# Attention and feed-forward layer: where two V products stand in the even heads

## What is computed

```
x = L0_attn_x
xn = _layernorm(x, axis=-1)
x = x + _L0_attn_ref(xn, Wq, bq, Wk, bk, Wv, bv, Wo, bo) + _L0_ffn_ref(xn, gate, up, down and their scales)

q = (x @ Wq + bq).reshape(b, h, t, dh)
k = (x @ Wk + bk).reshape(b, t, h, dh).transpose(0, 2, 3, 1)
v = (x @ Wv + bv).reshape(b, t, h, dh).transpose(0, 2, 1, 3)
logits = jnp.einsum('bhtd,bhds->bhts', q, k) * scale
weights = jax.nn.softmax(logits + mask, axis=-1)       # causal mask
out = jnp.einsum('bhts,bhsd->bhtd', weights, v)
return out.transpose(0, 2, 1, 3).reshape(b, t, h * dh) @ Wo + bo
```

## Time and profile before

| | |
|---|---|
| median of three runs | 1229.3 us |
| the profiled execution, its own time | 1229.01 us |
| its span, first to last instruction | 1227.2 us |
| TensorE matmuls busy | 1213.9 us (99%) |
| VectorE busy | 858.6 us (70%) |
| ScalarE busy | 746.6 us (61%) |
| GpSimd busy | 747.2 us (61%) |
| TensorE on the chain that ended last | 92% |
| granted TensorE clock | 1.0 |

### The profile page before, as it was taken

How to read it: one execution, slowest core, us unless ns; L and a number is a source line. 1 busy time by engine, 2 the same in 40 slices (tenths; PEclk the granted TensorE clock), 3 DMA queues, 4 the chain that set the end, 5 groups by cost and what they waited for, 6 DMA issues and landing times.

```text
span 1227.2 us, 20579 instructions
## 1 busy us (share of the span) xinstructions
PE 1213.9 (99%) x7556; PEld 1077.2 (88%) x7556; DVE 858.6 (70%) x1674; ACT 746.6 (61%) x1548; POOL 747.2 (61%) x796
## 2 busy tenths in 40 slices
PE   9999999999999999999999999999999999999998
PEld 8888888888889898889999988899898889899987
DVE  7777777776677666766677766677666766677775
ACT  6644444444576667666667765676666666666764
POOL 7445555553576767446767772676767446767763
PEclk9999999999999999999999999999999999999999
DMA  7100000000000001110000012010001100000001
GB/s 170 32 7 14 14 14 7 27 1 9 14 13 14 17 23 31 35 31 14 27 14 14 14 31 65 14 48 14 14 27 31 48 1 13 27 14 14 14 6 35
DMA packets 57346, 29.86 MB, mean 24 GB/s; under 512 B 16288, under 2 KB 57248, under 8 KB 57248
## 3 DMA queue, kind: packets, MB, share of 16 engines
q1 hardware_dynamic: 55888, 27.49, 8.1%
q10 hardware_dynamic: 1360, 1.06, 0.3%
HBM read 26.44 MB, written 2.10 MB: 23 GB/s over the span
## 4 chain that ended last, share of the span: by engine, by line
PE 92%; ACT 2%; POOL 2%; DVE 2%; issue 1%; DVEq 0%; ACTq 0%; POOLq 0%
PE ps L41 27%; PE ps L43 27%; PE ps L42 27%; PE ps L1164 10%; PE ps L1026 1%; PE ps L1005 1%; DVE pt_lo L877 1%; POOL probs L736 1%; ACT q_all L413 0%; ACT pt_hi L491 0%; ACT probs L505 0%; ACT wq_hi L403 0%; POOL wq_lo L622 0%; POOL inv_sum L733 0%; DVE probs L958 0%
## 5 line engine op out<-in xcount | busy, mean ns | idle before, releaser
L736 POOL TENSOR_TENSOR probs<-probs,inv_sum 128x128 f32<-128x128 f32 (+7 forms) x256 | 293.6, 1147 | 20.1
L733 POOL TENSOR_TENSOR inv_sum<-row_sum,minus_one 128x1 f32<-128x1 f32 x256 | 140.5, 549 | 225.2 <-ACT probs L505 224.2
L505 ACT ACTIVATE probs<-probs,neg_max 128x128 f32<-128x128 f32 (+7 forms) x256 | 198.8, 777 | 92.2 <-DVE neg_max L958 90.3
L491 ACT ACTIVATE pt_hi<-ps 128x512 fp32r<-128x512 f32 (+3 forms) x384 | 173.7, 488 | 93.0 <-PE ps L1164 90.4
L877 DVE TENSOR_TENSOR pt_lo<-ps,pt_hi 128x512 fp32r<-128x512 f32 (+3 forms) x384 | 200.9, 551 | 16.0 <-ACT pt_hi L491 15.8
L958 DVE CUSTOM_DVE_ANT_0 probs<-ps,mask_row 128x128 f32<-128x128 f32 (+7 forms) x256 | 192.1, 750 | 6.4
L1164 PE MATMUL ps<-ident,probs 128*128 128x128 f32 x1152 | 168.7, 273 | 4.1 <-DVE pt_lo L877 2.1
L717 POOL TENSOR_TENSOR hid_lo<-act_buf,hid_hi 128x512 fp32r<-128x512 f32 x64 | 82.7, 1293 | 139.3 <-ACT hid_hi L445 139.3
L1164 PEld LDWEIGHTS ps<-ident,probs 128*128 128x128 f32 x1152 | 133.7, 141 | 17.4 <-issue 7.2
L43 PE MATMUL ps<-pt_hi,v_lo 128*128 128x512 f32 (+3 forms) x386 | 133.0, 345 | 0.0
L42 PE MATMUL ps<-pt_lo,v_hi 128*128 128x512 f32 (+3 forms) x386 | 132.9, 344 | 0.0
(11 more groups left out here) (154 smaller groups left out, 3377.1 us busy)
## 6 DMA issues: line engine op xcount, KB each, us to landing
wq_in<-in_wq SPq DMA_DIRECT2D x63, 128.0 KB, 2.4
kv_in<-in_wk SPq DMA_DIRECT2D x16, 256.0 KB, 2.6
wo_in<-in_wo SPq DMA_DIRECT2D x32, 128.0 KB, 2.1
kv_in<-in_wv SPq DMA_DIRECT2D x32, 128.0 KB, 2.4
out<-acc SPq DMA_DIRECT2D x7, 256.0 KB, 2.6
acc<-in_x SPq DMA_DIRECT2D x2, 512.0 KB, 5.4
raw<-in_gate SPq DMA_DIRECT2D x16, 64.0 KB, 1.8
raw<-in_up SPq DMA_DIRECT2D x16, 64.0 KB, 2.0
```

The lines of the kernel that those rows point to most:

```text
L491: nc.scalar.activation(pt_blocks(pt_hi, i, ch), T[at % 2][:, 0:blocks * P].rearrange("p (a b) -> p a b", b=P), ACT.Copy).then_inc(pt_hi_do ...
L505: nc.scalar.activation(row, row, ACT.Exp, bias=neg_max[:, s % 16:s % 16 + 1], scale=-1.0, accum_out=row_sum[:, s % 16:s % 16 + 1]).then_in ...
L733: nc.gpsimd.tensor_tensor(inv_sum[:, at], row_sum[:, at], minus_one[:], ALU.pow).then_inc(inv_done, 1)
L736: nc.gpsimd.tensor_tensor(row, row, inv_sum[:, at].to_broadcast([P, (tile_of(h, i) + 1) * P]), ALU.mult).then_inc(probs_done, 1)
```

## The change

In the even heads V0 moves from EARLY to LATE in step 4, behind the probabilities' products, and V1 moves from LATE in step 4 to EARLY in step 5, behind that step's scores. In head 30 V1 moves in the same way, and K1+ moves from EARLY to LATE in step 5, directly behind V1. The order of the jobs among each other stays.

```diff
-        EVEN = {0: {EARLY: "K0"}, 1: {FIRST: "K1"}, 2: {EARLY: "O0a"}, 3: {LATE: "O0b"}, 4: {EARLY: "V0", LATE: "V1"},
+        EVEN = {0: {EARLY: "K0"}, 1: {FIRST: "K1"}, 2: {EARLY: "O0a"}, 3: {LATE: "O0b"}, 4: {LATE: "V0"}, 5: {EARLY: "V1"},
                 6: {FIRST: "O1a"}, 7: {FIRST: "O1b"}}
...
-        JOBS[NH - 2] = {**EVEN, 5: {EARLY: "K1+"}, 6: {EARLY: "O1a"}, 7: {EARLY: "O1b"}}
+        JOBS[NH - 2] = {**EVEN, 5: {EARLY: "V1", LATE: "K1+"}, 6: {EARLY: "O1a"}, 7: {EARLY: "O1b"}}
```

## The result

The change makes the kernel slower: 1249.3 us, the median of four runs (1249.15 to 1249.78), against 1229.15 us before. The ratio is 1.0164, with a 95% interval from 1.0152 to 1.0176. Forecast were 1248.0 us and a range of 1244.4 to 1252.5. The profiled execution of after took 1249.15 us with a span of 1247.3, so 20.1 us more than that of before.

A forecast was written before the change was run, and what follows sets the result against it. TensorE bounds the kernel, by its work plus its waits. Waits of 19.9 us in 14 heads and 1.6 in head 30, less 2.5 gained, add 19.0 to 1229.0: 1248.0 us, range 1244.4 to 1252.5.

The forecast's parts named there:

- The gain: Heads 6, 14 and 22: V0 no longer waits 0.82 us for GpSimd's vw_lo, 2.5 us saved in all.
- the three waits: V0's waits for GpSimd's vw_lo in heads 6, 14 and 22, 0.82 us each, forecast to go.
- The copy of 1.58 us: From the slot behind a V product to the next product on shared bank M, ScalarE and VectorE free: 1.58 us.
- Waits A and B: Even heads, bank M: V1 waits 0.20 us behind V0 (A), O1a waits 1.22 us behind V1 (B).
- The sum: Waits of 14 heads 19.9 us, head 30 1.6, less gain 2.5: net +19.0 us.
- The upper bound: 1252.5 us, if bank M's copy takes 1.73 us instead of 1.58 at both waits of 14 heads and head 30.
- The busy time: TensorE's busy time stays near 1214 us while the span grows to about 1246.
- The copies did not stay hidden: Faster rival: bank M's copies stay hidden, only the vw_lo wait goes, 1226.5 us; chance 0.05 together with a mixed case.
- The copy did not queue behind the maximum of the scores: Slower rival: VectorE's maximum comes ahead of V1's v_lo, 0.95 us in each of 15 heads, 1262 us; chance 0.07.
- The clock did not fall: Rival: TensorE from O1a to head's end runs at 1.2 GHz in 15 heads, about 1318 us; chance 0.02.
- The rule on short idle spells: Skill page's warning: short idle spells from waiting for PSUM buffers can let TensorE's clock swing between two levels.
- The low bound: 1244.4 us, if half of the 7.2 us that 20 transposes waited with their weight loads went.

The follow-up runs named there:

- clearing GpSimd's queue alone: Kernel before, with splits of the next group's first Q weights moved from steps 1 and 3 to steps 3 and 5: 1226.2 us, ratio 0.9978.
- V1 ahead of the scores: The change with V1 moved ahead of step 5's scores, and K1+ in head 30 behind them: 1249.56 us, ratio 1.0168.
- V0 back: The change with V0 returned to its old place, EARLY in step 4, V1 and K1+ left as moved: 1247.44 us, ratio 1.015.
- the bank of its own: The change with V1 of heads 2 to 30 written to bank O instead of bank M, no instruction moved: 1230.7 us, ratio 1.0013.

## Why the prediction was right

*The gain.* 2.5 us were forecast from the earlier trace rows; the three waits are gone, and clearing GpSimd's queue alone gives 2.8 us (by the interval of its ratio, 1.6 to 3.8). Right.

*The copy of 1.58 us.* It was read at one place, head 30, and is 1.57 us at both places in head 4 of after. That ScalarE and VectorE are free in time was worked out from durations; the 1.05 us that VectorE idled before the second v_lo show it. Right, with 0.3 us more to spare than counted.

*Waits A and B.* 0.20 and 1.22 us forecast, 0.19 and 1.21 measured. K1+ waits 1.6 us as forecast. Their sum over the heads is the 22.1 us in the list of weight loads, 15 x 0.24 + 14 x 1.21 + 1.61; the rows of the weight loads count wait A as 0.24 us, where the starts give 0.19.

*The sum.* 19.0 us forecast, 20.1 measured in the profiled executions. The two waits of head 4 are 1.40 us together where 1.42 were forecast, 0.3 us less in 14 heads. What the sum lacked is that the products do not keep their lengths. In head 4 V1 takes 437.66 - 436.15 = 1.51 us where it took 1.45 before (432.97 to 434.42), and O1a takes 0.82 us (439.23 to 440.05, where the next scores start) where it took 0.79 in the kernel before (436.16 in the earlier trace rows to 436.95):

```profile
436.95 0.40 PE L41 MATMUL ps<-k_hi_even,q_hi 128*128 128x512 f32 x1
```

Both now start after a wait. The probabilities' products take 1.90 us where they took 1.88; they wait for nothing, but stand directly behind the narrow scores now, where V0 stood; V0 takes 1.46 for 1.47. Together this is 0.10 us in a head and 1.5 us in 15 heads, which with the 0.3 us less makes up the 1.1 us to about a tenth. The step that left it out is the one that moved the products with unchanged lengths (it kept 0.10 us for the start behind the scores, and took "V1 the same" as V0).

*The range.* That the time fell inside it owes something to luck. The upper bound stood for a copy of 1.73 us in place of 1.58, and the copy stayed at 1.57; the 1.1 us above the forecast came from a term that neither bound contained.

*The busy time.* I said that TensorE's busy time would stay near 1214 us. It rose to 1220.1. The number of matmuls is the same. The row of the four transposes ahead of O1a lasts 0.60 us. Before the change O1a started 0.36 us into it; ahead of a gap all 0.60 count as busy, 0.24 more. So of the 1.21 us before O1a the matmuls' row shows 0.97, and the weight load's row shows it all. This changed no term, since the terms were read from start to start.

*The rivals.* The copies did not stay hidden. The copy did not queue behind the maximum of the scores. The clock did not fall; stretches of after, as in the earlier trace rows:

```profile
420.00:1195.00 775.00, 760.16 (x4757) 674.87 (x4756) 526.70 (x1069) 500.82 (x1084) 489.02 (x547) 1.00 0.08 23
```

TensorE was idle for 14.84 of 775 us here, in gaps that come back every other head, and the granted clock stayed at 1.00, the 2.4 GHz level. The rule on short idle spells that the prediction cites (the Trainium skill, TensorE: Matmul & The Clock Gate, "A second HAM failure mode: psum-queue depth-cycling") is reported there of a bf16 kernel; it was not seen to act here: the clock stayed at its high level through gaps of 0.19 and 1.21 us in every other head.

*What could help later.* The low bound rested on the transposes' 7.2 us of waits shrinking. They stayed at 7.2.

## What to carry to other kernels

Where products share one PSUM bank, count the TensorE work between each two of them, and compare it with one measured turnaround of the bank (here 1.57 us from the slot behind a product to the next). A product that moves takes its distance from one neighbour and gives it to the other. Where the whole stretch is too short for two turnarounds, as the 1.74 us from V0 to O1a with the change, the sum of both waits follows from the stretch, and moving within it cannot help (V1 ahead of the scores). Where it is long enough, the place decides: in the kernel before 1.88 and 1.74 us hid both copies, and with V0 back the same work, split into 3.26 and 0.36, left the wait of 1.21 us. Another bank can help in either case, as long as the copies behind it are looked at too. And a wait of 2.5 us in three places is better cured at its source, the queue ahead of it, than by moving the waiting work in fifteen.

## What the runs showed of the hardware

A product that starts after a wait runs longer than the same product in the same place without one. V1 behind the scores of step 5 takes 1.51 us with the change, after a wait, and 1.40 in the bank of its own, without (434.86 to 436.26); O1a behind the four transposes takes 0.82 with the change, after a wait, and 0.79 in the kernel before, without. In the rows of V1 the first weight load starts 0.12 us ahead of its matmul where there is no wait (434.74), and together with it after one (436.15). That the late load is what costs the time fits these rows, but no run tests it by itself.

A wait of TensorE is not whole in the rows of the matmuls: they show 0.97 us of the 1.21 before O1a, and nothing of the 0.19 before V1. The rows of the weight loads show 1.21 and 0.24.
